# Expert layers: row buffers in rings of eight, gathers and scatters issued in groups of four

## The reference

```python
# layer 0: 8 experts, hidden width 512
top_w, top_idx = top_k(softmax(x_flat @ router_w.T), 2)
h = relu(einsum('tc,efc->tef', x_flat, w1) + b1)
y = einsum('tef,ecf->tec', h, w2) + b2
out = sum over the two picked experts of top_w * y

# layer 1: 16 experts, hidden width 256
topv, topi = top_k(x @ router_w.T + router_bias, 2); weights = softmax(topv)
mag, freq = einsum('td,ndh->tnh', fx, bank_mag), einsum('td,ndh->tnh', fx, bank_freq)
hidden = tanh(mag) * cos(softplus(freq) + 0.1 + bank_phase)
out = sum over the two picked experts of weights * (hidden @ bank_down)
out = out * rsqrt(mean(out * out) + 1e-6) * norm_w
```

## Time and profile before

| | us |
|---|---|
| median of the runs before | 829.02 |
| the profiled execution's own time | 832.29 |
| its span (first to last instruction) | 830.5 |
| TensorE busy | 542.7 (65%) |
| VectorE busy | 559.3 (67%) |
| GpSimd busy | 412.0 (50%) |
| ScalarE busy | 307.3 (37%) |
| mean granted TensorE clock | 0.808 of full speed |

### The profile page before, as it was taken

The page is one execution under the profiler, slowest core; times in us unless marked ns, Lnnn a source line. Parts: engine busy times, 40 slices in busy tenths (PEclk is TensorE's granted clock), DMA queues, the critical chain, the costliest instruction groups (busy, mean ns, idle before and its releaser), DMA issues.

```text
span 830.5 us, 8703 instructions
## 1 busy us (share of the span) xinstructions
PE 542.7 (65%) x1820; PEld 282.1 (34%) x1821; DVE 559.3 (67%) x1091; ACT 307.3 (37%) x616; POOL 412.0 (50%) x291
## 2 busy tenths in 40 slices
PE   3668889779888959418888881066505767376750
PEld 2313333333333324215556560033402222155530
DVE  5864698779598988493223335936794778866647
ACT  3365454464535623002222221272101555690003
POOL 0067879478777958025565651010005656046650
PEclk9869889798978989758999996567555999869875
DMA  4044345223222320361111114000101113311124
GB/s 157 0 149 158 129 132 196 69 79 118 86 71 84 127 76 26 139 282 39 42 41 41 40 39 126 0 1 0 52 0 28 40 38 38 96 45 42 44 68 120
DMA packets 36657, 63.51 MB, mean 76 GB/s; under 512 B 5202, under 2 KB 22164, under 8 KB 36116
## 3 DMA queue, kind: packets, MB, share of 16 engines
q1 hardware_dynamic: 30996, 51.64, 18.8%
q0 software_dynamic: 5632, 11.55, 5.7%
HBM read 53.99 MB, written 9.18 MB: 76 GB/s over the span
## 4 chain that ended last, share of the span: by engine, by line
PE 44%; DVE 29%; issue 9%; ACT 7%; DMA 4%; DVEq 4%; POOL 1%; another core or an unknown queue 1%; SPq 1%; ACTq 0%; POOLq 0%
PE ps L852 12%; PE ps L952 9%; PE ps L937 4%; DVE hs L1302 4%; PE ps L821 4%; PE ps L846 3%; DVE h_tok L1105 3%; PE ps L944 3%; DVEq L1359 2%; DVE prod L1312 2%; DVE p_hot L1193 2%; PE ps L1055 1%; DVE freq L1475 1%; PE ps L1036 1%; PE ps L769 1%
## 5 line engine op out<-in xcount | busy, mean ns | idle before, releaser
L427 POOL TENSOR_TENSOR bu<-uT,b_sb 128x1024 f32<-128x1024 f32 x64 | 149.0, 2347 | 33.8 <-DVE uT L1282 33.8
L852 PE MATMUL ps<-prod,cst 128*128 128x512 f32 x256 | 140.4, 699 | 0.5 <-DVE yT L1322 0.3
L395 POOL DMA_INDIRECT y_dram<-ys,rows_i x88 | 87.6, 995 | 88.7 <-DVE ys L1532 36.7
L389 POOL DMA_INDIRECT xl<-h_dram,rows_i x88 | 90.2, 1025 | 50.5 <-issue 20.5
L559 ACT ACTIVATE ps<-dtT,neg_a 128x512 f32<-128x512 f32 x128 | 85.1, 684 | 52.0 <-DVE hs L1302 50.3
L438 POOL TENSOR_TENSOR prod<-hs,c_sb 128x1024 f32<-128x1024 f32 x32 | 75.1, 2347 | 56.6 <-DVE hs L1302 49.2
L1302 DVE TENSOR_TENSOR_SCAN hs<-ps,bu 128x512 f32<-128x512 f32 x64 | 74.2, 1208 | 25.6 <-ACT ps L559 22.9
L852 PEld LDWEIGHTS ps<-prod,cst 128*128 128x128 f32 x256 | 54.1, 222 | 89.8 <-issue 86.4
L1302 DVE TENSOR_TENSOR_SCAN hs<-ps,carry,bu 128x512 f32<-128x512 f32 x64 | 78.1, 1268 | 6.6 <-ACT ps L559 6.0
L846 PE MATMUL ps<-bc_f,sel_f 32*128 32x512 f32 x64 | 44.2, 777 | 50.5 <-DVE prod L1312 50.5
L1036 PE MATMUL ps<-mf_s,xt 128*128 x96 | 56.7, 678 | 20.6 <-issue 9.4
(11 more groups left out here) (220 smaller groups left out, 944.1 us busy)
## 6 DMA issues: line engine op xcount, KB each, us to landing
b_sb<-b_rows SPq DMA_DIRECT2D x32, 512.0 KB, 4.7
c_sb<-b_rows SPq DMA_DIRECT2D x32, 256.0 KB, 3.7
w_s<-in_w SPq DMA_DIRECT2D x17, 256.0 KB, 4.3
mf_s<-in_mf SPq DMA_DIRECT2D x1, 4096.0 KB, 17.0
h_dram<-h_tok SPq DMA_DIRECT2D x8, 256.0 KB
b_s<-in_b SPq DMA_DIRECT2D x1, 2048.0 KB, 7.9
phase_s<-in_phase SPq DMA_DIRECT2D x1, 2048.0 KB, 22.9
down_s<-in_down SPq DMA_DIRECT2D x1, 2048.0 KB, 7.2
```

Source lines behind the costliest of these rows:

```text
L389: pool.indirect_dma_start(xl[:, j % XR, :], None, h_dram[l], bass.IndirectOffsetOnAxis(ap=rows_i[:, 0, j:j + 1], axis=0)).then_inc(loaded[ ...
L395: pool.indirect_dma_start(y_dram[l], bass.IndirectOffsetOnAxis(ap=rows_i[:, 1, j:j + 1], axis=0), ys[:, j % XR, :], None).then_inc(saved[l ...
L427: nc.gpsimd.tensor_tensor(bu[:, g % RING, :, :], uT[:, c % 2, :, :], b_sb[:, k % BRING, g % 2, :].unsqueeze(1).broadcast_to([P, ND, CHUNK] ...
L852: last = nc.tensor.matmul(bank(Y_BANK + d), ident, prod[:, g % RING, d, :], start=n == 0, stop=n == NS - 1)
```

## The change

Both rings get eight buffers in both layers (`XR = 8`, where layer 1's `ys1` had `GT = 4`). In layer 0 GpSimd first issues eight gathers, and then for every four tiles b to b+3: the gathers of tiles b+8 to b+11, then the scatters of tiles b to b+3. The waits are the same with the ring's new length: a gather waits for the transpose of the tile eight earlier, `bias_down` and `copy_y` for the scatter eight tiles earlier. The loops are cut to the new length: TensorE's in layer 0 has a body of 8 tiles and four trips (12 tiles and three trips before) with four tiles written out around it; VectorE's in layer 0 has a body of 8 tiles and three trips (4 and eight before), that in stage C 8 tiles and four trips (4 and ten before). To make room, the table's working arrays (`p_hot` and what follows) share their place with `y0`, and `hd1` and `ht1` lie behind `ys1`.

```diff
--- before.py
+++ after.py
@@ -34,9 +34,9 @@
 ST0 += -ST0 % 4
 ST1 = (2 * T + E1 * (P - 1)) // P
 ST1 += -ST1 % 4
-XR = 4
+XR = 8
+BATCHED = 4
 PICKS = 2 * NTILE
-LEAD = 6
 GT = 4
 NG = ST1 // GT
 LN_EPS = 1e-5
@@ -218,12 +218,13 @@
         hp0, e = place("hp0", [P, 2, F0], at=e)
         ht0, e = place("ht0", [P, 2, F0], at=e)
         ys0, e = place("ys0", [P, XR, C], at=e)
+        y0_at = e
         y0 = [None, None]
         y0[0], e = place("y0a", [P, NTILE, C], at=e)
         y0[1], e = place("y0b", [P, NTILE, C], at=e)
         xn_tok = y0[1]
 
-        p_hot, e = place("p_hot", [P, PICKS, P], BF16, at=e)
+        p_hot, e = place("p_hot", [P, PICKS, P], BF16, at=y0_at)
         j_rows, e = place("j_rows", [P, PICKS, 2 * ST1], BF16, at=e)
         j_hot, e = place("j_hot", [P, PICKS, ST1], BF16, at=e)
         slot_f, e = place("slot_f", [P, 2, NTILE], at=e)
@@ -239,9 +240,10 @@
 
         xl1, e = place("xl1", [P, XR, C], at=h_at)
         xt1, e = place("xt1", [P, 2, P], at=e)
+        assert e <= hT_at
+        ys1, e = place("ys1", [P, XR, C], at=h_at)
         hd1, e = place("hd1", [P, 2, H1], at=e)
         ht1, e = place("ht1", [P, 2, H1], at=e)
-        ys1, _ = place("ys1", [P, GT, C], at=h_at)
         assert e <= hT_at
         fabs, e = place("fabs", [P, 2, GT, H1], at=hT_at)
         hold = route[:, 0:2 * GT, :].rearrange("p (q a) h -> p q a h", q=2)
@@ -446,11 +448,13 @@
                     products(2 * k - 1)
             products(STEPS - 1)
             weigh_tiles(0, ST0)
-            for j in range(ST0 + LEAD):
-                if j < ST0:
+            for j in range(XR):
+                take_rows(0, j, xl0)
+            for b in range(0, ST0, BATCHED):
+                for j in range(b + XR, min(b + XR + BATCHED, ST0)):
                     take_rows(0, j, xl0)
-                if j >= LEAD:
-                    put_rows(0, j - LEAD, ys0)
+                for j in range(b, b + BATCHED):
+                    put_rows(0, j, ys0)
 
             for c in range(NCHUNK):
                 ts = slice(c * CT, (c + 1) * CT)
@@ -967,13 +971,23 @@
             turn_x(0, xl0, 2, 0, 2)
             up0(1, 1)
             turn_h0(0, 0)
-            with pe.Fori(0, (ST0 - 4) // 12) as i:
-                for k in range(12):
-                    j, u = i * 12 + (k + 2), k % 2
-                    turn_x(0, xl0, j + 1, i * 3 + (k + 3) // XR, (k + 3) % XR)
+            for j in (2, 3):
+                turn_x(0, xl0, j + 1, 0, j + 1)
+                up0(j, j % 2)
+                turn_h0(j - 1, 1 - j % 2)
+                down0(j - 2, j % 2)
+            with pe.Fori(0, (ST0 - XR) // XR) as i:
+                for k in range(XR):
+                    j, u = i * XR + (k + 4), k % 2
+                    turn_x(0, xl0, j + 1, i + (k + 5) // XR, (k + 5) % XR)
                     up0(j, u)
                     turn_h0(j - 1, 1 - u)
                     down0(j - 2, u)
+            for j in (ST0 - 4, ST0 - 3):
+                turn_x(0, xl0, j + 1, (j + 1) // XR, (j + 1) % XR)
+                up0(j, j % 2)
+                turn_h0(j - 1, 1 - j % 2)
+                down0(j - 2, j % 2)
             n = ST0
             turn_x(0, xl0, n - 1, (n - 1) // XR, (n - 1) % XR)
             up0(n - 2, 0)
@@ -1041,7 +1055,7 @@
             with pe.Fori(0, NG // 2 - 1) as i:
                 for k in range(2 * GT):
                     j = i * (2 * GT) + k
-                    turn_x(1, xl1, j + 1, i * 2 + (k + 1) // XR, (k + 1) % XR)
+                    turn_x(1, xl1, j + 1, i + (k + 1) // XR, (k + 1) % XR)
                     up1(j, k % GT)
             for j in range(ST1 - 2 * GT, ST1):
                 if j + 1 < ST1:
@@ -1536,20 +1550,20 @@
             copy_ht(0, 0)
 
             def down_steps(j0, g, stored):
-                for k in range(GT):
+                for k in range(XR):
                     hidden(j0 + (k + 2), g + (k + 2) // GT, k % 2)
                     copy_ht(j0 + (k + 1), (k + 1) % 2)
                     copy_y(j0 + k, stored, k)
 
             down_steps(0, 0, None)
-            with dve.Fori(0, ST1 // GT - 2) as i:
-                down_steps(i * GT + GT, i + 1, i + 1)
-            for j in range(ST1 - GT, ST1):
+            with dve.Fori(0, ST1 // XR - 2) as i:
+                down_steps(i * XR + XR, i * 2 + 2, i + 1)
+            for j in range(ST1 - XR, ST1):
                 if j + 2 < ST1:
                     hidden(j + 2, (j + 2) // GT, j % 2)
                 if j + 1 < ST1:
                     copy_ht(j + 1, (j + 1) % 2)
-                copy_y(j, j // GT, j % GT)
+                copy_y(j, j // XR, j % XR)
 
             nc.vector.tensor_tensor(mod[:, 1, :, GB, :], mod[:, 1, :, GB, :], nw_s[:, :].unsqueeze(1).broadcast_to([P, BATCH, C]),
                                     ALU.mult).then_inc(S["dve_chain"], 1)
```

## The result

| | before | after |
|---|---|---|
| median of four runs, us | 827.28 (823.17 to 830.86) | 846.83 (844.61 to 850.01) |
| the profiled execution, us | 832.29 | 848.3 |
| its span, us | 830.5 | 846.5 |
| A: first gather to last scatter, us | 371.47 to 501.42, 129.9 | 369.66 to 509.98, 140.3 |
| B: first gather to first scatter, us | 630.07 to 731.50, 101.4 | 638.45 to 748.20, 109.8 |

The ratio is 1.0241, 95% interval 1.0177 to 1.0305; the forecast was 827.7 us in 815 to 838. The 827.28 us are the three executions behind 829.02 and a fourth, of 823.17. B as measured here runs from GpSimd's first gather to its first scatter, the two rows that every trace has; it takes in the first steps of C.

What follows compares the result with a forecast made beforehand. It took TensorE's late results, held by something unknown, as the bound, with GpSimd next in stage A. Loops (-0.9) and stage C's ring (-0.4) summed to -1.3 us, from 829.02 to 827.7 us, range 815 to 838.

Steps and rivals of the forecast that it cites:

- Order in groups of four, A: Stage A: scatters standing behind up to four gathers (5.1 us) make nobody wait; cost 0, 5.1 us a group if uncovered.
- the slower rival: Stage A: GpSimd's unbroken issuing holds TensorE's results, so grouped gathers lengthen pauses; +13 us, 842 us, chance 0.12.
- point of decision: Stage A: longer pauses start when a run of eight issues (10.3 us) outlasts TensorE's work on hand.
- The sign: Stages A and C: similar TensorE instruction rates, 9.1 and 8.0 per us, tie the pauses to TensorE's own instruction stream.
- The argument against the rival: Stage A pause: GpSimd would have stopped anyway, since its next scatter depends on the held result.
- Ring of eight, B: Stage B: gathers run four tiles further ahead for a TensorE that doesn't wait for them; gain 0.
- Scatter ring of eight and gather ring, A: Stage A: longer rings remove no binding wait; 0 each, at most 23.8 us for scatters and 2.1 us for gathers.
- The two faster rivals: Stage A: rings did bind, 808 us, chance 0.10; or pauses come half as often, 818 us, chance 0.08.
- Loops, and the ring in C: Stage C: six fewer VectorE loop trips gain 0.9 us, the longer ring 0.4 us; A's loops 0.
- The 0.4 us of it for an old scatter: Stage C: VectorE's one wait for an old scatter, 0.4 us, goes with the ring of eight.
- The port rule: Stage B: VectorE's port lock stretches gathers, so a deeper ring could gain up to 4.8 us; taken as 0.

Runs made afterwards that it cites:

- e11: The change itself again, unedited, against the kernel before on a chip without pauses: 790.04 us, ratio 0.9918.
- e18: Changed kernel with layer 0 alternating gather and scatter, layer 1's gathers as plain SyncE loads of neighbouring rows; chip with pauses: 818.66 us, ratio 0.9869.
- e5: The change itself again, unedited, against the kernel before on a chip with pauses: 845.03 us, ratio 1.0152.
- e12: Changed kernel with layer 0 alternating gather and scatter again, rings of eight kept; chip without pauses: 794.33 us, ratio 0.996 to the kernel before.
- e15: Changed kernel with layer 0 alternating again and layer 1's gathers four tiles ahead, rings of eight kept; chip without pauses: 796.64 us, ratio 1.0006.
- e9: Changed kernel using expert 0 for every tile, no register loads on TensorE or VectorE; chip without pauses: 774.86 us, ratio 0.9733.

## Why the prediction was wrong

**The step that failed** is "*Order in groups of four, A.* … Cost 0." It asked who waits for a scatter that stands behind four gathers, and that answer holds: the first scatter came late (17.6 us after the first gather, where 12.9 were before and 15.2 were reckoned) and no wait for an old scatter followed. The step didn't ask what an unbroken run of issues does to the engines that wait for nothing of GpSimd. That was known as a suspicion, and is priced in the slower rival: 4 x 2.34 us free plus 5.1 us of gathers, 14.5 us a group. Measured are 13.97 us a group, with a held piece of 4.5 to 5 us, and 10.4 us for the stage where the rival had 13. Its point of decision, a run of eight issues (10.3 us), was set too high: runs of six, 7.3 us from 451.81 to 459.15, were already longer than TensorE's work on hand.

**The reason for the low chance was wrong**: "I take this as a sign that the pauses go with TensorE's own instruction stream." The sign was that stages A and C ran at 9.1 and 8.0 recorded instructions of TensorE per us. e11 runs stage A at (98 + 97) / 15 = 13.0 per us; and in e18 TensorE's unchanged stream of stage B has no pauses. Both stages are full of GpSimd's issues, and that fits both paces; shown is it in B alone, as no run took the scatters of A or C away on a chip with pauses. The argument against the rival ("GpSimd would have stopped for want of work in any case") was true and didn't bear on it: that GpSimd stops because it has nothing to issue, and that most results come free some 1.2 us after it stops, can be the two halves of one cycle. On that reading a pause in the old order lasts until GpSimd runs dry, and gathers, which need nothing of TensorE, put that off.

**Ring of eight, B**: "Gathers of B run four tiles further ahead, for a TensorE that doesn't wait for them: 0." It cost 8.3 us. TensorE indeed doesn't wait for gathers, but beside 15 issues in a row, in place of six, it stood twice, for 5.18 us the second time (661.01). No rival had this, though the slower one's mechanism applies word for word. That GpSimd's gathers, their issuing or their transfers, are the cause in B is shown by e18; that the ring's length is what makes it worse than before rests on three traces (2.50 us at most before, 5.18 in the changed kernel, 7.44 in e5), since four ahead never met a chip with pauses.

**Scatter ring of eight and gather ring, A**: 0 each was right. "Remote" before `ys` is still there at 26.0 us with eight buffers, and e12 and e15 are within 0.4% of before. The two faster rivals are out on chips with pauses. A does run at GpSimd's 2.57 us a tile on chips without (e12), and so, I suppose, does the kernel before, which was not profiled there.

**Loops, and the ring in C**: -1.3 us forecast, -0.3 measured in C's 72.5 and 72.2; too small to tell. The 0.4 us of it for an old scatter stood under "remote", the label that the prediction itself had distrusted in A.

**The port rule.** The gain of up to 4.8 us in B, which the prediction weighed by a rule of the Trainium skill (SBUF — State Buffer, Who interferes with whom), didn't come: B's gathers took 48.4 us in place of 51.4, and the stage got longer. The same section says that only the shared port pair causes contention, and gives TensorE no part in it. The runs add a wait that this rule wouldn't lead one to look for: on the chips with pauses results of TensorE reached their readers up to some 4.5 us late while GpSimd issued indirect transfers. Whether that happens at the ports or elsewhere no run shows. Another page explains why it is easy to miss. By the Trainium skill (Perfetto Trace Analysis, Tensor Engine Instruction) the end of a TensorE instruction in a profile is estimated from its size, and its semaphore is sent only when PSUM has acknowledged the write. The trace agrees that the recorded end isn't when a reader gets the result: a transpose "over" at 455.89 reached ScalarE at 460.39. It doesn't show at which of the steps between the time was spent.

**Open** are four things: what in a chip decides whether it has the pauses; whether GpSimd's making of descriptors or the software queue's transfers hold the results (e18 took both away from B); whether register loads are held too, in A and B; and how A and B share the loss on one chip, since the order and the ring's length were never undone one at a time beside the change on a chip with pauses.

## What to carry to other kernels

When two engines that don't need each other both stop, look what a third was doing, and until when: here ScalarE's long waits in the groups of stage A ended 1.17 to 1.30 us after an issue of GpSimd. While a kernel shows such pauses, don't give an indirect-DMA engine longer unbroken runs, neither by grouping nor by a deeper ring; rows that can be had by plain loads on another queue are worth moving. And a loss or gain of 1 to 2% may belong to the chip: the same edit was 2.4 and 1.5% slower in two comparisons and 0.8% faster in a third, on another chip, so compare on more than one before keeping either.

## What the runs showed of the hardware

The same program took 796 us on some chips and 827 to 831 us on others, with a mean granted clock of 0.797 in the profile after and 0.826 in e11, and the difference lies in the stretches in which GpSimd issues indirect transfers: A 104.5 or 140.3 us (all first e11, then the profile after), B 96.4 or 109.8, C 61.7 or 72.2 for the changed kernel, 59.6 us together where the spans differ by 58.5. Issued back to back, an indirect transfer costs GpSimd 1.25 to 1.30 us in stage A in either order; some gathers of stage B take longer (1.62 us and the 0.30 to the next, at 665.49 and 669.90 in the changed kernel). Loading a tile's expert number into registers on TensorE and VectorE costs some 10 us in stage B on chips without pauses (86.2 us in e9 against 96.4 in e11), more than any part of this change gained.
